# First attention of a four-stage block: the probabilities turned in 32x32 blocks on VectorE and exchanged through memory, with the order around the mixing changed

## Chip, cores and metric

One NeuronCore of one Trainium2 chip runs the whole program. The metric is the device time of one execution in microseconds (us), the median of three runs. TensorE has two clock levels, 1.2 and 2.4 GHz. A granted clock of 1.00 in the tables is the higher one.

## The reference

Sixteen tiles of 128 tokens with 512 features pass four residual stages, each behind a layer norm without gains. The change is in the first:

```
x = x + xattn(layernorm(x), ctx)           # 2048 tokens; this case
x = x + ffn(layernorm(x))                  # 512-1024-1024-512
x = x + xattn_rope(layernorm(x), ctx)
x = x + mlp_and_experts(layernorm(x))

def xattn(h, c):                           # H = 16 heads, D = 128; per batch row 128 queries, 128 keys
    q, k, v = h @ Wq, c @ Wk, c @ Wv       # 512x2048, 256x2048, 256x2048
    q, k = rmsnorm(q, gq), rmsnorm(k, gk)  # per head
    attn = softmax(q k^T / sqrt(D))
    return (attn @ v) @ Wo                 # 2048x512
```

All is float32. A large product is computed as three products of a rounded part (`_hi`) and a rest (`_lo`) of each operand.

## The kernel before

The first attention takes 32 steps, `s = 0..31`. The weights of 8 heads fit at a time, so steps 0 to 15 do the 16 tiles with heads 0 to 7, and steps 16 to 31 the same tiles with heads 8 to 15. In a step the 8 heads are two groups of `G = 4`, `g = 0, 1`. Each group fills one PSUM bank of 512 columns at each stage of the work. The second half of the weights comes in around steps 14 to 16: ScalarE writes the rounded part (`split_hi`), VectorE the rest (`split_lo`).

The order on each engine is written out by hand, one function `step(s)` for each, and semaphores join them (`at(name, s)` is the count that `name` has after step `s`). A step works on two tiles at once: scores, softmax, mixing and output for tile `s`, and keys, queries and values for tile `s + 1`. It also turns the normalised x of tile `s + 2`.

TensorE's order in a plain step is: `score(s,0)`, `output(s-1,1)`, `score(s,1)`, `keys(s+1,0)`, `turn_p(s,0)`, `keys(s+1,1)`, `mix(s,0)`, `queries(s+1,0)`, `turn_p(s,1)`, `queries(s+1,1)`, `mix(s,1)`, `output(s,0)`, `turn_x(s+2)`, `values(s+1,0)`, `values(s+1,1)`. A product of queries or an output is 12 matmuls of 128x512, one of keys or values is 6.

The path of one group through a step:
- `maxima` (VectorE) waits for `score` and gives the bias. `exps` (ScalarE) writes four heads of unscaled probabilities and their sums. `normalise` (VectorE) takes the reciprocal and multiplies.
- `turn_p` (TensorE) transposes the four 128x128 blocks into PSUM, `copy_pT` (VectorE) copies them to `pT_sb`, and `mix` multiplies with the values.
- `split_o` on ScalarE and then on VectorE makes `oT_hi` and `oT_lo` for `output`. The second group mixes into bank 1, in which the next `score(s+1,0)` writes, so that one waits for `oT_lo1`.

Queries and keys of tile `s + 1` are turned without TensorE: VectorE transposes 32x32 blocks (`turn_q`, `norm_and_turn_k`) into `blocks`, SyncE (SP) stores them to `turned` in HBM (`send`) and loads them back in another order (`bring`) as `qkT`. The norm of k needs its squares (`square` on ScalarE) and GpSimd's `mean`. `square` of q waits for `turn_q`, since both read the same bank.

SP issues its transfers in the order written, and a wait holds all that stand behind it.

Of the kernel before, what the change touches and what calls it, by code (L numbers as in the profile page):

```python
# [90 lines left out]
def l0_attention(place, sem, bank, ident, ident_in, x, ctxT, wq, wk, wv, wo, gq, gk, turned, x1):  # L91
# [14 lines left out]
    spots |= spots_of(200, "qkT1 4")  # L106
# [8 lines left out]
    def parts(name, shape):  # L115
# [21 lines left out]
    pT_sb = [sb(f"pT_sb{g}", [P, G * P], F32) for g in range(2)]  # L137
# [16 lines left out]
        s_turn y_begun y_ready y_added wq0_staged wv_staged wk_staged wq1_staged wo0_staged wo1_staged""".split()  # L154
    names += [f"{n}{g}" for g in range(2) for n in """q_made k_made v_made q_blocks k_blocks qk_stored qk_loaded v_copied q_squared
        k_squared q_rms k_rms scored bias_ready exped normed p_turned pT_copied mixed oT_hi oT_lo""".split()]
# [75 lines left out]
    def sync(sp, ahead):  # L232
# [33 lines left out]

        def step(s, second_half=True, storing=True):
# [111 lines left out]
    def tensor(pe, ahead):  # L379
# [63 lines left out]
        def step(s):  # L443
# [7 lines left out]
            if now == STEPS - 1:  # L451
                ahead["turn_x"](pe, 0, 3)
            if now == FIRST:
# [3 lines left out]
            if there(s):  # L457
                turn_p(s, 0)
            if there(s + 1):
                keys(s + 1, 1)  # L460
            if now == STEPS - 1:
                ahead["hidden1"](pe, 0, 0)
            if there(s):
                mix(s, 0)
            if there(s + 1):
# [3 lines left out]
            if there(s):  # L469
                turn_p(s, 1)  # L470
            if now == STEPS - 1:
                pe.wait_ge(*at("v_copied1", s))
                ahead["hidden1"](pe, 0, 1)
            if there(s + 1):
                queries(s + 1, 1)
            if there(s):
                mix(s, 1)
# [4 lines left out]
            if there(s):  # L482
                output(s, 0)
            if now == STEPS - 1:
                ahead["hidden1"](pe, 0, 2)
            if there(s + 2):
                turn_x(s + 2)
            if there(s + 1):
                values(s + 1, 0)
                values(s + 1, 1)  # L490
            if now == STEPS - 2:
# [7 lines left out]
    def scalar(act, ahead):  # L499
# [38 lines left out]
        def step(s):  # L538
# [20 lines left out]
            if now == FIRST:  # L559
                split_hi(act, "wq1", 0)  # L560
            if there(s):
# [4 lines left out]
            if now == NB - 1:  # L566
                split_hi(act, "wv0", 1)
                split_hi(act, "wv1", 1)
            if now in (0, NB):
                split_hi(act, "wo1", now // NB)  # L570
            if there(s + 1):
                square(s + 1, 0, "q")
            if now == NB - 2:
                split_hi(act, "wq0", 1)
            if now == FIRST:
                split_hi(act, "wv0", 0)
                split_hi(act, "wv1", 0)
            if now == STEPS - 2:
                ahead["split_x_hi"](act, 0, 0)
            if now == STEPS - 1:  # L580
                ahead["hidden_hi"](act, 0, 0, 0)
            if there(s + 1):
                square(s + 1, 1, "q")
# [4 lines left out]
            if now == STEPS - 2:  # L588
                ahead["split_x_hi"](act, 0, 1)
            if now == STEPS - 1:  # L590
                ahead["hidden_hi"](act, 0, 0, 1)
                ahead["split_hi"](act, 4)
            if there(s + 2):
                split_xT(s + 2)
# [14 lines left out]
    def vector(dve, ahead):  # L609
# [79 lines left out]
        def step(s, first_half=False):  # L689
# [8 lines left out]
            if there(s - 1):  # L698
                add_y(s - 1)
            if now == STEPS:  # L700
# [8 lines left out]
            if there(s):  # L709
                copy_pT(s, 0)  # L710
# [24 lines left out]
            if there(s):  # L735
                split_o(s, 0)
# [6 lines left out]
            if there(s):  # L743
                copy_pT(s, 1)
# [8 lines left out]
            if now == NB - 2:  # L753
# [1920 lines left out]
```

## Time and profile before

| | |
|---|---|
| median of 3 runs | 1987.45 us (1985.17 to 1993.48) |
| span of the profiled execution | 1985.1 us |
| TensorE matmul busy | 1935.9 us, 98% |
| VectorE busy | 1315.2 us, 66% |
| ScalarE busy | 742.2 us, 37% |
| GpSimd busy | 564.5 us, 28% |
| mean granted clock | 0.996 |
| first attention, first `score` to last `score` of group 0 | 30.77 to 724.93 us |

The span is the time from the first to the last instruction of one execution. An engine's share is a mean over four stages that differ, so it doesn't say what a change of one stage is worth. That has to be read in the steps of the stage. The 32 steps follow each other with the same pattern, so one step can be read for nearly all.

### The profile page before, as it was taken

What the parts mean: (1) busy time and instruction counts of PE and PEld (TensorE: products, weight loads), DVE (VectorE), ACT (ScalarE), POOL (GpSimd) and SP (SyncE); (2) the same over time, 40 slices, a digit from 0 to 9 for tenths busy, and PEclk for the clock granted to TensorE, in tenths of its full rate; (3) what the DMA queues carried; (4) which work ended last, traced back from release to release, by engine and by line L of the source; (5) the groups of instructions that cost most, each with busy time, mean ns of one, the idle gap of its engine ahead of it and who ended that gap; (6) DMA issues with size and microseconds to landing.
All of it is one profiled execution on the core that took longest, in us unless ns stands there. A gap on an engine that the chain in (4) does not pass through costs nothing. (4 is left out here: it accounts for less than half of the span.)

```text
span 1985.1 us, 35876 instructions
## 1 busy us (share of the span) xinstructions
PE 1935.9 (98%) x13552; PEld 1562.9 (79%) x13552; DVE 1315.2 (66%) x2493; ACT 742.2 (37%) x2275; POOL 564.5 (28%) x705
## 2 busy tenths in 40 slices
PE   6999999899999999999999899999999999999999
PEld 4888888778888878888888677777688888888887
DVE  6656655665555654343345599988868878888786
ACT  5555455654555543111122344444433222122211
POOL 3322222322223425310121343433310222322231
PEclk9999999999999999999999899999999999999999
DMA  6632333433444433020122100000112546555654
GB/s 233 221 103 90 99 114 108 165 112 117 137 148 143 144 107 128 27 80 32 32 69 93 63 28 18 21 23 19 54 54 70 191 154 210 192 192 167 201 163 160
DMA packets 126294, 222.39 MB, mean 112 GB/s; under 512 B 17392, under 2 KB 72688, under 8 KB 126192
## 3 DMA queue, kind: packets, MB, share of 16 engines
q1 hardware_dynamic: 102480, 134.01, 20.5%
q0 software_dynamic: 23712, 87.04, 13.2%
q8 instruction: 61, 1.00, 0.2%
q14 instruction: 41, 0.34, 0.1%
HBM read 170.16 MB, written 50.86 MB: 111 GB/s over the span
## 5 line engine op out<-in xcount | busy, mean ns | idle before, releaser
L2385 POOL DMA_INDIRECT m_ring<-in_table,m_row x128 | 127.3, 994 | 370.0 <-DVE l_x_all L2498 264.1
L48 PE MATMUL four_banks<-l_yT_hi,m_hi 128*128 128x512 f32 x512 | 199.4, 389 | 0.0
L48 PE MATMUL four_banks<-l_yT_lo,m_hi 128*128 128x512 f32 x512 | 199.2, 389 | 0.0
L1147 DVE TENSOR_SCALAR f_relu<-bank,f_b 128x512 f32<-128x512 f32 x64 | 48.0, 750 | 166.3 <-ACT f_h_hi L1090 166.3
L529 ACT ACTIVATE prob<-four_banks,mx,rms 128x128 f32<-128x128 f32 x256 | 114.0, 454 | 114.3 <-DVE mx L667 114.3
L328 POOL TENSOR_TENSOR rms<-ssq,constants 128x4 f32<-128x4 f32 x128 | 34.9, 273 | 391.9 <-ACT junk_k L518 237.9
L1090 ACT ACTIVATE f_h_hi<-bank,f_b 128x512 fp32r<-128x512 f32 x64 | 44.2, 690 | 255.6 <-PE bank L48 255.6
L331 POOL TENSOR_TENSOR rms<-rms,constants 128x4 f32<-128x4 f32 x128 | 130.1, 1016 | 10.0
L48 PEld LDWEIGHTS four_banks<-l_yT_hi,m_hi 128*128 128x128 f32 x512 | 96.1, 188 | 20.1 <-issue 0.2
L48 PEld LDWEIGHTS four_banks<-l_yT_lo,m_hi 128*128 128x128 f32 x512 | 96.1, 188 | 20.0
L2362 ACT ACTIVATE m_act_of<-m_dot,l_ln_y 128x2 f32<-128x2 f32 x64 | 19.0, 297 | 238.6 <-DVE m_junk L2488 238.6
L682 DVE TENSOR_TENSOR oT_lo<-four_banks,oT_hi 128x512 fp32r<-128x512 f32 x64 | 44.2, 691 | 95.5 <-ACT oT_hi L536 95.5
L48 PE MATMUL bank<-f_h_hi,f_w_hi 128*128 128x512 f32 x256 | 100.7, 394 | 1.0 <-DVE f_relu L1147 0.9
L48 PE MATMUL bank<-f_h_lo,f_w_hi 128*128 128x512 f32 x256 | 99.7, 389 | 0.0
L48 PE MATMUL bank<-m_hi,m_prod_hi 128*128 128x512 f32 x256 | 99.7, 389 | 0.0
L48 PE MATMUL bank<-f_h_hi,f_w_lo 128*128 128x512 f32 x256 | 99.7, 389 | 0.0
L2488 DVE SCALAR_TENSOR_TENSOR m_junk<-m_x_in,l_ln_y,m_ring 128x512 bf16<-128x512 f32 x128 | 92.0, 751 | 11.6 <-DMA m_ring<-in_table,m_row 10.5
L48 PE MATMUL four_banks<-l_yT_hi,m_gate 128*128 128x512 f32 x256 | 99.6, 389 | 0.0
L48 PE MATMUL bank<-m_hi,m_prod_lo 128*128 128x512 f32 x256 | 99.6, 389 | 0.0
L48 PE MATMUL four_banks<-l_yT_hi,m_up 128*128 128x512 f32 x256 | 99.6, 389 | 0.0
L48 PE MATMUL bank<-m_down,m_prod_hi 128*128 128x512 f32 x256 | 99.6, 389 | 0.0
L48 PE MATMUL four_banks<-wo_hi,oT_hi 128*128 128x512 f32 x240 | 99.4, 414 | 0.0
(316 smaller groups left out, 5410.2 us busy)
## 6 DMA issues: line engine op xcount, KB each, us to landing
turned<-blocks SPq DMA_DIRECT2D x64, 512.0 KB, 2.9
qkT<-turned SPq DMA_DIRECT2D x64, 512.0 KB, 4.3
f_stage<-in_w POOLq DMA_DIRECT2D x14, 512.0 KB, 4.6
f_x_in<-x SPq DMA_DIRECT2D x18, 256.0 KB, 3.5
ctx_in<-in_ctxT SPq DMA_DIRECT2D x32, 128.0 KB, 2.6
x_in<-in_x SPq DMA_DIRECT2D x16, 256.0 KB, 2.7
x<-xres SPq DMA_DIRECT2D x16, 256.0 KB, 2.1
x<-l_x_all SPq DMA_DIRECT2D x16, 256.0 KB
```

The costliest lines, as they stand in the source:

```text
L48: mm = pe.matmul(out, st, mv, start=first and n == 0, stop=last and n == len(terms) - 1)
L328: pool.tensor_tensor(rms[g][:, 1, own], ssq[g][:, 0 if of == "q" else 1, :], constants[:, 0, own], ALU.add).then_inc(S["eps_added"], 1)
L331: pool.tensor_tensor(rms[g][:, 0, own], rms[g][:, 1, own], constants[:, 1, own], ALU.pow).then_inc(S[f"{of}_rms{g}"], 1)
L529: a = act.activation(prob[g][:, j, :], bank[(1, 3)[g]][:, j * P:(j + 1) * P], ACT.Exp, bias=mx[g][:, 1, j:j + 1], scale=rms[g][:, 0, j:j + 1],
L682: dve.tensor_tensor(flat(oTp[g][1]), bank[(0, 1)[g]][:], flat(oTp[g][0]), ALU.subtract).then_inc(S[f"oT_lo{g}"], 1)
L1090: act.activation(out, bank[HB[m % 2]][:], ACT.Relu, bias=b12[:, layer, m:m + 1]).then_inc(S["h_hi"], 1)
L1147: dve.tensor_scalar(relu[m % 2][:], bank[HB[m % 2]][:], b12[:, layer, m:m + 1], 0.0, ALU.add, ALU.max).then_inc(S["relu_ready"], 1)
L2362: act.activation(act_of[:, t, k.start:k.stop], dot[:, t, k.start:k.stop], ACT.Silu, scale=ln[:, 2 * t + 1:2 * t + 2]).then_inc(S["silued"], 1)
L2385: pool.indirect_dma_start(ring[slot][:], None, table, bass.IndirectOffsetOnAxis(ap=row[:, tile_of(g), k:k + 1], axis=0)).then_inc(S[f"got{ ...
L2488: d = dve.scalar_tensor_tensor(junk[:, k % PER, :], x_in[t % 2][:], ln[:, 2 * t:2 * t + 1], ring[slot][:, 0:DM], ALU.subtract, ALU.mult, a ...
```

## The change

The probabilities are no longer turned by TensorE. ScalarE's `exps` writes the keys of a head in another order (key `4a + b` at place `32b + a`). VectorE's `normalise` then transposes 32x32 blocks into `dealt`. SP stores `dealt` to `shares` in HBM (`deal`) and loads it back in another order into `pT_sb` (`take`), which is laid out in four pieces of 32 queries. `turn_p` and `copy_pT` go.

The order changes with it. On TensorE the turn of the next x and `values(s+1,0)` stand ahead of `mix(s,0)`, `values(s+1,1)` between the mixings, and `output(s,0)` at the end. `output(s-1,1)` keeps its place. On ScalarE and VectorE both `split_o` come behind the work on tile `s + 1`, and so do some conversions of weights. `add_y` moves behind the second maxima. On SP, `deal` and `take` of each group stand ahead of `send` and `bring`.

```diff
@@ memory and names
+    spots |= spots_of(200, "qkT1 4 dealt 2")
-    pT_sb = [sb(f"pT_sb{g}", [P, G * P], F32) for g in range(2)]
+    dealt = sb("dealt", [P, 4, G, 32], F32)
+    pT_sb = [sb(f"pT_sb{g}", [P, 4, G, 32], F32) for g in range(2)]
+    shares = nc.dram_tensor("shares", (2, 4, P, P), F32).ap()
@@ SP
+        def deal(s, g):
+            sp.wait_ge(*at(f"p_blocks{g}", s))
+            sp.dma_start(shares[g].rearrange("p (j b) r -> (p j) (b r)", b=4), dealt[:].rearrange("p b h i -> p (b h i)")
+                         ).then_inc(S["p_stored"], 16)
+
+        def take(s, g):
+            sp.wait_ge(S["p_stored"], 16 * (2 * s + g + 1))
+            if there(s - 1):
+                sp.wait_ge(*at(f"mixed{g}", s - 1))
+            sp.dma_start(pT_sb[g][:].rearrange("k p h i -> k p (h i)"), shares[g].rearrange("p k r -> k p r")
+                         ).then_inc(S[f"p_loaded{g}"], 16)
...
                 load_ctx(s + 2)
+            if there(s):
+                deal(s, 0)
+                take(s, 0)
             if storing:
                 store(s - 1)
             if second_half and there(s + 3):
                 load_x(s + 3)
+            if there(s):
+                deal(s, 1)
+                take(s, 1)
@@ TensorE
         def queries(s, g):
...
+            elif there(s - 1):
+                pe.wait_ge(*at("exped1", s - 1))
         def values(s, g):
...
+            elif there(s - 1):
+                pe.wait_ge(*at("v_copied0", s - 1))
-        def turn_p(s, g):
-            pe.wait_ge(*at(f"normed{g}", s))
+        def mix(s, g):
+            pe.wait_ge(S[f"p_loaded{g}"], 16 * (s + 1))
+            pe.wait_ge(*at(f"v_copied{g}", s))
             if g == 0 and there(s - 1):
                 pe.wait_ge(*at("y_added", s - 1))
-            turn((0, 1)[g], flat(prob[g]), f"p_turned{g}")
-
-        def mix(s, g):
-            pe.wait_ge(*at(f"pT_copied{g}", s))
-            pe.wait_ge(*at(f"v_copied{g}", s))
             for j in range(G):
                 c = slice(j * P, (j + 1) * P)
-                mm = pe.matmul(bank[(0, 1)[g]][:, c], v_sb[g][:, c], pT_sb[g][:, c], start=True, stop=True)
+                out = bank[(0, 1)[g]][:, c].rearrange("d (p i) -> d p i", p=4)
+                mm = pe.matmul(out, v_sb[g][:, c], pT_sb[g][:, :, j, :], start=True, stop=True)
@@ ScalarE
             for j in range(G):
-                a = act.activation(prob[g][:, j, :], bank[(1, 3)[g]][:, j * P:(j + 1) * P], ACT.Exp,
+                scores = bank[(1, 3)[g]][:, j * P:(j + 1) * P].rearrange("q (a b) -> q a b", b=4)
+                a = act.activation(prob[g][:, j, :].rearrange("q (b a) -> q a b", b=4), scores, ACT.Exp,
@@ VectorE
-            dve.tensor_tensor(prob[g][:], prob[g][:], den[g][:, 1, :].unsqueeze(2).to_broadcast([P, G, P]),
-                              ALU.mult).then_inc(S[f"normed{g}"], 1)
-
-        def copy_pT(s, g):
-            dve.wait_ge(*at(f"p_turned{g}", s))
-            dve.tensor_copy(pT_sb[g][:], bank[(0, 1)[g]][:]).then_inc(S[f"pT_copied{g}"], 1)
+            then(dve.tensor_tensor(prob[g][:], prob[g][:], den[g][:, 1, :].unsqueeze(2).to_broadcast([P, G, P]), ALU.mult))
+            if g == 1 or there(s - 1):
+                dve.wait_ge(S["p_stored"], 16 * (2 * s + g))
+            dve.transpose(dealt[:], blocks_of(flat(prob[g]))).then_inc(S[f"p_blocks{g}"], 1)
```

The steps in the new order, each in a plain step and then in the odd ones (`now` is the step's number):

```
TensorE  score(s,0) output(s-1,1) score(s,1) keys(s+1,0) keys(s+1,1) queries(s+1,0) queries(s+1,1)
         turn_x(s+2) values(s+1,0) mix(s,0) values(s+1,1) mix(s,1) output(s,0)
ScalarE  exps(s,0) exps(s,1) square k0 k1 q0 q1 of s+1, split_xT(s+2) split_o(s,0) split_o(s,1)
         copy_v(s+1,0) copy_v(s+1,1) split_ctx(s+2)
         15: split_hi wv0, wv1 between the squares of q0 and q1
         14: split_hi wk0, wk1, wq0 between split_o(s,0) and split_o(s,1);  0 and 16: split_hi wo1 there
VectorE  maxima(s,0) normalise(s,0) maxima(s,1) add_y(s-1) layer_norm(s+2) normalise(s,1)
         norm_and_turn_k, turn_q of (s+1,0) and of (s+1,1), split_xT(s+2) split_o(s,0) statistics(s+3) split_o(s,1)
         15: split_lo wq1 and, 0 and 16: split_lo wo0, behind normalise(s,1), as before
         15: split_lo wv0 ahead of norm_and_turn_k(s+1,1);  14: split_lo wk0, wk1 behind split_o(s,0)
31       TensorE: the first two products of the next stage ahead of mix(s,0), the third between the mixings
```

## Rows read from the trace of the kernel before

**Rows 1.** Windows view of step 8: busy time of each engine, clock, DMA share.

```profile
187.94:210.00 22.06, 22.06 (x165) 17.95 (x164) 13.30 (x30) 11.18 (x54) 6.30 (x12) 1.00 0.31 100
```

**Rows 2.** Timeline of step 8, TensorE: start us, us, engine, line, tiles.

```profile
187.94 1.08 PE L420 MATMUL four_banks<-qkT 128*32 128x128 f32 x32
...
194.17 0.39 PE L48 MATMUL bank<-wk_hi,ctx_lo 128*128 128x512 f32 x1
194.40 0.60 PE L382 MATMUL four_banks<-ident,prob 128*128 128x128 f32 x4
...
195.07 0.40 PE L48 MATMUL bank<-wk_lo,ctx_hi 128*128 128x512 f32 x1
...
196.23 1.05 PE L434 MATMUL four_banks<-pT_sb,v_sb 128*128 128x128 f32 x8
...
210.00 1.08 PE L420 MATMUL four_banks<-qkT 128*32 128x128 f32 x32
```

**Rows 3.** Timeline of step 8, the other engines.

```profile
191.68 0.21 ACT L529 ACTIVATION_READ_ACCUMULATOR prob<-four_banks,mx,rms 128x1 f32 x1
...
193.55 0.69 DVE L664 TENSOR_REDUCE mx<-four_banks 128x4 f32<-128x512 f32 x1
...
194.47 0.46 ACT L529 ACTIVATE prob<-four_banks,mx,rms 128x128 f32<-128x128 f32 x1 [2.58 <-DVE mx L667]
...
196.23 0.28 ACT L518 ACTIVATE junk_k<-bank 128x128 bf16<-128x128 f32 x1
...
197.73 1.01 POOL L331 TENSOR_TENSOR rms<-rms,constants 128x4 f32<-128x4 f32 x1
...
199.53 1.12 DVE L657 SCALAR_TENSOR_TENSOR k_sb<-bank,rms,gains 128x128 f32<-128x128 f32 x4
...
204.27 0.67 DVE L650 STREAM_TRANSPOSE blocks<-four_banks 128x512 f32<-128x512 f32 x1
204.98 0.28 ACT L518 ACTIVATE junk_q<-four_banks 128x128 bf16<-128x128 f32 x1 [1.81 <-DVE blocks L650]
...
205.46 2.83 SPq L264 DMA_DIRECT2D qkT<-turned  x2
...
206.00 0.62 ACT L536 ACTIVATE oT_hi<-four_banks 128x512 fp32r<-128x512 f32 x1
...
206.65 0.69 DVE L682 TENSOR_TENSOR oT_lo<-four_banks,oT_hi 128x512 fp32r<-128x512 f32 x1 [1.70 <-ACT oT_hi L536]
```

**Rows 4.** Lines by form, and line 1901 with its shortest, median and longest ns.

```profile
L660 DVE STREAM_TRANSPOSE blocks<-k_sb 128x512 f32<-128x512 f32 x64 | 45.5, 711 | 2.2
L678 DVE COPY pT_sb<-four_banks 128x512 f32<-128x512 f32 x64 | 43.0, 673 | 22.3 <-PE four_banks L382 22.3
L2461 DVE TENSOR_TENSOR m_best<-m_best,m_total 128x32 f32<-128x32 f32 x4 | 0.8, 192 | 0.1
L1901 DVE TENSOR_SCALAR l_ang<-l_pos x4: 197/427/1276, 1040.4 to 1042.6; 128x32 f32<-128x32 f32 x4
```

**Rows 5.** DMA issues of the page: KB each, median us from issue to landing.

```profile
turned<-blocks SPq DMA_DIRECT2D x64, 512.0 KB, 2.9
qkT<-turned SPq DMA_DIRECT2D x64, 512.0 KB, 4.3
```

**Rows 6.** Timelines at steps 0, 1, 15, 16, and conversions by form.

```profile
30.77 1.08 PE L420 MATMUL four_banks<-qkT 128*32 128x128 f32 x32
...
55.58 1.08 PE L420 MATMUL four_banks<-qkT 128*32 128x128 f32 x32
...
365.01 1.08 PE L420 MATMUL four_banks<-qkT 128*32 128x128 f32 x32 [0.34 <-DMA qkT<-turned]
...
392.23 1.08 PE L420 MATMUL four_banks<-qkT 128*32 128x128 f32 x32 [2.87 <-DMA qkT<-turned]
...
L203 ACT ACTIVATE wv_hi<-stage 128x1024 fp32r<-128x1024 f32 x4 | 4.1, 1101 | 0.0
L207 DVE TENSOR_TENSOR wq_lo<-stage,wq_hi 128x2048 fp32r<-128x2048 f32 x3 | 6.9, 2287 | 1.6 <-ACT wq_hi L203 1.6
```

More of the change, by code:

```diff
@@ L88, in norm_statistics, with l0_attention @@
     then(rsqrt_steps(dve, then, ln[:, tiles, 1], ln_t[:, 0, tiles], ln_t[:, 1, tiles]))
-def l0_attention(place, sem, bank, ident, ident_in, x, ctxT, wq, wk, wv, wo, gq, gk, turned, x1):
+def l0_attention(place, sem, bank, ident, ident_in, x, ctxT, wq, wk, wv, wo, gq, gk, turned, shares, x1):
     H, D, HALF, G = 16, 128, 8, 4
@@ L153, in l0_attention @@
         g_loaded stats_ready ln_eps ln_ready xn_ready xT_turned xT_hi xT_lo ctx_hi ctx_split set stored eps_added
-        s_turn y_begun y_ready y_added wq0_staged wv_staged wk_staged wq1_staged wo0_staged wo1_staged""".split()
+        s_turn y_begun y_ready y_added p_stored wq0_staged wv_staged wk_staged wq1_staged wo0_staged wo1_staged""".split()
     names += [f"{n}{g}" for g in range(2) for n in """q_made k_made v_made q_blocks k_blocks qk_stored qk_loaded v_copied q_squared
-        k_squared q_rms k_rms scored bias_ready exped normed p_turned pT_copied mixed oT_hi oT_lo""".split()]
+        k_squared q_rms k_rms scored bias_ready exped p_blocks p_loaded mixed oT_hi oT_lo""".split()]
     PIECES = ("wq0", "wq1", "wk0", "wk1", "wv0", "wv1", "wo0", "wo1")
@@ L452, in step @@
                 ahead["turn_x"](pe, 0, 3)
+                ahead["hidden1"](pe, 0, 0)
+                pe.wait_ge(*at("v_copied1", s))
+                ahead["hidden1"](pe, 0, 1)
             if now == FIRST:
@@ L456, in step @@
                 keys(s + 1, 0)
-            if there(s):
-                turn_p(s, 0)
-            if there(s + 1):
                 keys(s + 1, 1)
[L461 to L465, printed above, removed]
                 queries(s + 1, 0)
@@ L468, in step @@
                 ahead["turn_x"](pe, 0, 0)
[L469 to L473, printed above, removed]
             if there(s + 1):
                 queries(s + 1, 1)
-            if there(s):
-                mix(s, 1)
             if now == STEPS - 2:
@@ L481, in step @@
                 ahead["turn_x"](pe, 0, 1)
[L482 to L485, printed above, removed]
             if there(s + 2):
@@ L489, in step @@
                 values(s + 1, 0)
+            if there(s):
+                mix(s, 0)
+            if there(s + 1):
                 values(s + 1, 1)
+            if now == STEPS - 1:
+                ahead["hidden1"](pe, 0, 2)
+            if there(s):
+                mix(s, 1)
+                output(s, 0)
             if now == STEPS - 2:
@@ L560, in step @@
                 split_hi(act, "wq1", 0)
+            if now == STEPS - 1:
+                ahead["hidden_hi"](act, 0, 0, 0)
+            if there(s + 1):
+                square(s + 1, 0, "q")
+            if now == NB - 1:
+                split_hi(act, "wv0", 1)
+                split_hi(act, "wv1", 1)
+            if now == FIRST:
+                split_hi(act, "wv0", 0)
+                split_hi(act, "wv1", 0)
+            if now == STEPS - 2:
+                ahead["split_x_hi"](act, 0, 0)
+            if there(s + 1):
+                square(s + 1, 1, "q")
+            if now == STEPS - 1:
+                ahead["hidden_hi"](act, 0, 0, 1)
+            if now == STEPS - 2:
+                ahead["split_x_hi"](act, 0, 1)
+            if there(s + 2):
+                split_xT(s + 2)
             if there(s):
@@ L565, in step @@
                 split_hi(act, "wk1", 1)
-            if now == NB - 1:
-                split_hi(act, "wv0", 1)
-                split_hi(act, "wv1", 1)
+                split_hi(act, "wq0", 1)
             if now in (0, NB):
                 split_hi(act, "wo1", now // NB)
[L571 to L583, printed above, removed]
             if now is not None and AHEAD_FROM < now <= AHEAD_FROM + 4:
@@ L697, in step @@
                 ahead["split_x_lo"](dve, 0, 2)
-            if there(s - 1):
+            if now == STEPS:
                 add_y(s - 1)
-            if now == STEPS:
                 ahead["hidden_lo"](dve, 0, 0, 2)
@@ L708, in step @@
                 ahead["split_x_lo"](dve, 0, 3)
-            if there(s):
-                copy_pT(s, 0)
+            if there(s - 1) and now != STEPS:
+                add_y(s - 1)
             if now == FIRST:
@@ L742, in step @@
                 split_lo(dve, "wq1", 0)
-            if there(s):
-                copy_pT(s, 1)
+            if now == NB - 1:
+                split_lo(dve, "wv0", 1)
             if there(s + 1):
@@ L765, in step @@
                 ahead["hidden_lo"](dve, 0, 0, 0)
-            if there(s):
-                split_o(s, 1)
+                ahead["hidden_lo"](dve, 0, 0, 1)
             if now == STEPS - 2:
@@ L773, in step @@
                 split_xT(s + 2)
+            if there(s):
+                split_o(s, 0)
+            if now == NB - 2:
+                split_lo(dve, "wk0", 1)
+                split_lo(dve, "wk1", 1)
+            if now in (0, NB):
+                split_lo(dve, "wo1", now // NB)
             if first_half:
                 statistics(s + 3)
+            if there(s):
+                split_o(s, 1)
             if now == NB - 2:
                 split_lo(dve, "wq0", 1)
-            if now == STEPS - 1:
-                ahead["hidden_lo"](dve, 0, 0, 1)
         all_steps(dve, step, first_half=True)
@@ L2578, in build @@
         done, programs0 = l0_attention(place, sem, bank, ident, a["ident"], a["x"], a["ctxT"], a["wq0"], a["wk0"], a["wv0"], a["wo0"],
-                                       a["gq"], a["gk"], turned, x1)
+                                       a["gq"], a["gk"], turned, shares, x1)
         over, ahead1, programs1 = l0_ffn(place, sem, bank, ident, done, x1, a["w1"], a["b1"], a["w2"], a["b2"], a["w3"], a["b3"], x2)
-        free = [s for n, s in done.items() if not n.rstrip("012345").endswith(("loaded", "staged", "stored"))]
+        free = [s for n, s in done.items() if not n.rstrip("012345").endswith(("loaded", "staged", "stored")) or n.startswith("p_")]
         over["semaphores"] = ranges_of([s.num for s in free])
```

14 lines of the change are left out of this document (removed).

## The prediction

> **What bounds the kernel now.** I read first the windows view of one plain step of the attention (step 8), to see which engine has no slack [rows 1]: TensorE is busy for the whole 22.06 us, VectorE for 13.30, ScalarE for 11.18, the DMA engines for 31%, at a granted clock of 1.00. Then TensorE's timeline of that step [rows 2]: it begins with a `score` at 187.94 and the next begins at 210.00; every later step up to the last has this 22.06, except those in which the second half of the weights is put in place. So in this stage only two things move the end: TensorE work taken out, and any wait put in. The weight loads and matmuls of a product follow each other every 0.23 us (194.17 to 194.40 is one such interval); a turn of four transposes at 194.40, with the next product's second matmul at 195.07, takes 0.67 less one interval of 0.23, that is 0.44 us. Last I read the timeline of the other engines in the same step [rows 3], because the new order only pays if they deliver as early as TensorE then asks. Below, t is the time after the step's first `score` (187.94).
>
> **What leaves TensorE.** Two `turn_p` a step: 2 x 0.44 = 0.88 us. What TensorE alone would then need is 22.06 - 0.88 = 21.18 us. The mixing reads its moving operand in four pieces of 32 columns; `score` already reads `qkT` in that form, and I price this at nothing. The products that are moved keep their cost.
>
> **What VectorE gets.** Two copies of 0.67 go, two 32x32-block transposes of 0.71 come [rows 4], so its sum stays. Only their places matter. The first transpose takes the time that `add_y` had in front of the second maxima: exps 0 end at t = 3.95 (191.68 + 0.21), reciprocal, product and transpose bring VectorE to about t = 5.6, and `maxima(s,1)` began at t = 5.61 before. So exps 1 still begin at t = 6.53, the squares of k at 8.29, and GpSimd's power for k ends at 10.80 [rows 3].
>
> **The chain that then decides.** `norm_and_turn_k(s+1,0)` began at t = 11.59, directly behind other VectorE work (its row shows no idle time). The first split of o leaves that place, so it can begin when GpSimd is done, at 10.85. From there to the second `turn_q` were 4.74 us (199.53 to 204.27), 0.6 of them `copy_pT`, which goes: 4.14. The second q blocks begin at 14.99 and are ready at 15.70 (before: 17.04, the start of ScalarE's squares at 204.98). ScalarE's queue is now squares of q 1, split of xT, split of o 0. The squares occupy 1.02 us (204.98 to 206.00), so xT begins at 16.72. Two 512-element activations of 0.62 in a row I space at 0.5, since the end of one overlaps the next: o 0 begins at 17.22 and is out at 17.87. VectorE subtracts xT meanwhile and then o 0 in 0.69: `oT_lo0` is there at about 18.65, and `output(s,0)` begins at 18.7. TensorE would be ready for it at 21.18 - 12 x 0.23 - 0.09 = 18.33. It waits 0.4 us. The new period is 18.7 + 2.76 + 0.09 = 21.55 us, a gain of **0.5 us a step** instead of 0.88. The second half of o follows in time: mixing 1 ends at about 18.5, and its low part is out near 20.2, before the next `score` at 21.55.
>
> **The exchange through memory.** The block transpose of g = 1 ends at t = 10.1. The store is 256 KB, half of `turned`; the issues of SP land after 2.9 us for the 512 KB store and 4.3 for the 512 KB load back [rows 5]. I take 2.4 + 3.6, with the full 2.9 + 4.3 as the upper bound and nothing as the lower: the probabilities land at 16.2, at most 17.4, and mixing 1 is due at 17.4 (its matmuls of 1.05 end at 18.5, row 196.23). For g = 0 the blocks are ready at 5.7, landed at 12 to 13, due at 15.2. Hidden, without a margin at the upper bound. On SP, `take(s,1)` holds the queue until about 12.6 + 0.5. Behind it stands `send(s+1,0)`, whose blocks are ready at 13.4, so it loses nothing. The second `send` and the first `bring` go out at 15.8 and 16.3 instead of 17.1 and 17.5 (205.46), and q and k land near 20.6, before the `score` at 21.55. The time that SP waits for each store delays `store` and `load_x` only, which nobody waits for closely.
>
> **The other new waits.** The second transpose waits until the first store has read `dealt`: landed at t = 8.1, asked for at 9.4. `queries(s+1,1)` waits for exps 1, done at 8.4, asked for at about 10.6. `values(s+1,0)` waits for a copy of the step before. None costs anything; the first would hold VectorE, and all of the k and q work behind it, from a store of 3.7 us on.
>
> **The exps.** They now write with a step of 32 elements (128 bytes). No ScalarE row shows such a write. Lower bound: nothing. Upper bound: the elements take twice their time. A square of 128 elements takes 0.28 and an activation of 512 takes 0.62 [rows 3], so 128 elements are (0.62 - 0.28)/3 = 0.11 us, on top of 0.46. Eight exps stand in the chain (four in front of `maxima(s,1)`, four behind), so that bound adds 0.88 us to the period. The nearest row is on VectorE: line 1901 writes 32 elements with a step of 16 bytes in 197 ns at its shortest, and a 32-element operation with contiguous output takes 192 [rows 4]. Doubled it would be 33 ns more, and it is 5. I take nothing.
>
> The Trainium skill (SBUF — State Buffer, "Door 1: The DMA port swizzle") says that SBUF works in lines of 16 bytes, and that each access which crosses to a new line pays. Every element of the new write does that. By it the sum would be the upper bound instead of nothing, and the change would lose; the VectorE row speaks against it for writes, and no row here tests ScalarE.
>
> **Steps that are not plain.** In three steps around the half the weights are replaced, and the change moves these conversions too. Before, the step from 365.01 to 392.23 took 27.22, 5.2 too much, for a late `qkT` [rows 6]; its three neighbours lost 1.5 together (periods of 22.25, 22.46 and 22.98) and step 0 2.75 (its first `score` at 30.77, the next at 55.58): 9.5 in all. In the new order I estimate:
> - step 14: three conversions (1.1 us for each half of `wk` as for `wv` [rows 6], about 1.9 for `wq` with twice the elements) stand ahead of the second split of o, which the next `score` needs. It comes at about 22.9, 1.3 late.
> - step 15: `wv` is converted behind the squares of q 0, which wait for q blocks that come at 15.5, behind `wq1_lo` (2.29 us, VectorE). `values` wants it at 13.9 and gets it at 17.7. `wv0_lo` stands ahead of the second k, the second q blocks come at 21.3, output 0 at 24.3: 5.5 lost. The late `qkT` is hidden behind that.
> - step 16: `wo0_lo` (of the same size) ahead of k: 2.5. Step 0 alike, 4.
>
> Together 13.3 against 9.5: 4 lost. In the first steps weights and exchange share the DMA engines, 2 us. In the last step the mixings wait for their transfers with little in front of them, 1 us.
>
> **Sum.** 28 plain steps x 0.5 = -14; +4, +2, +1: **-7 us**. The profiled execution spans 1985.1 us, the median of the runs is 1987.45 (2.3 around the span and within the spread of 8 us), so **1980 us**, within 0.5% (10 us, about what a measurement of this kernel can tell from no change). Its own range: 1973 to 1988.
>
> **Rivals.**
> 1. *Slower: the scattered write of the exps.* Place: the eight exps ahead of the squares of k. Each 0.01 us of an exp costs 0.08 a step. From 0.46 to 0.52 the plain step is back at 22.06, and with the 7 us of the odd steps the kernel is slower than before from about 0.03 us per exp. At the upper bound the period is 22.43: 28 x 0.37 = +10, +7: 2005 us. For it: every exp is ahead of everything. Against: the VectorE row.
> 2. *TensorE stays the bound.* If GpSimd or the two ScalarE instructions behind the last squares come 0.4 us earlier than I put them, the whole 0.88 counts: 28 x 0.88 = 25, less 7: 1969 us. Against it: each link is a row of this step.
> 3. *The probabilities come late.* It decides where store and load of g = 1 need over 7.3 us from the transpose. 1 us later than that puts output 0 at 19.2, the period at 22.1, and only the odd steps count: 1995 us. For it: the loads in steps with weight traffic. Against: the DMA engines are busy for 31% in a plain step.
>
> **Chances.** Forecast 0.50, rival 1 0.27 (spread over 1990 to 2006), rival 2 0.13, rival 3 0.10. Faster than 1977.5: rival 2 and a quarter of the forecast, 0.26. Slower than 1997.4: two thirds of rival 1 and a fifth of rival 3, 0.20. Between: 0.54. The range 1966 to 2005 takes in all bounds but the ends of the tails.
>
> **What the new profile should show.** A plain step of 21.5 to 21.6 us between first `score`s. No row of `turn_p`. TensorE idle 0.3 to 0.5 us once a step, ahead of `output(s,0)`, released by VectorE's `oT_lo`. ScalarE's exps at 0.46 us (rival 1: 0.5 or more). No idle time ahead of the mixings with a DMA as releaser (rival 3). Steps 14 to 16 as 23, 27 and 24 us. I am wrong if the exps are longer, if the mixings wait for the transfer, or if the wait ahead of `output(s,0)` is absent.

## The result, and the profile after

| | before | after |
|---|---|---|
| median of 8 runs each | 1989.44 us (1985.17 to 1993.48) | 1999.02 us (1995.17 to 2001.48) |
| span of the profiled execution | 1985.1 us | 1999.7 us |

The ratio of after to before is 1.0039, 95% interval 1.0028 to 1.005: slower by some 8 us, where 0.4% faster was forecast. The profiled execution took 2001.48 us, at the upper end of its runs, so its 14.6 us of longer span overstate the loss, but they show where it lies.

From the page after: the exps of part 5 (busy us, mean ns of one, idle before), then the issues of part 6 (KB each, median us to landing).

```profile
L542 ACT ACTIVATE prob<-four_banks,mx,rms 128x128 f32<-128x128 f32 x256 | 121.7, 582 | 184.1 <-DVE mx L680 184.1
...
turned<-blocks SPq DMA_DIRECT2D x64, 512.0 KB, 3.2
qkT<-turned SPq DMA_DIRECT2D x64, 512.0 KB, 4.1
shares<-dealt SPq DMA_DIRECT2D x64, 256.0 KB, 2.0
pT_sb<-shares SPq DMA_DIRECT2D x64, 256.0 KB, 2.8
```

The windows view after, columns as in [rows 1]: a plain step of the first half (8), one of the second half (18), and step 30, the last before the last.

```profile
212.69:234.37 21.68, 21.37 (x158) 17.25 (x157) 13.35 (x30) 10.96 (x54) 6.28 (x11) 1.00 0.46 149
441.83:464.03 22.20, 21.47 (x157) 17.25 (x157) 12.79 (x28) 10.96 (x54) 5.52 (x9) 1.00 0.50 162
...
704.67:737.17 32.50, 24.80 (x165) 19.77 (x165) 14.69 (x32) 11.27 (x54) 6.45 (x12) 0.89 0.37 126
```

In step 8 TensorE is busy for 0.7 us less than in [rows 1], and idle for 0.3 us. Step 30 has almost 8 us without TensorE, and a lower mean clock. (Counted from the first `score` at 30.77, the plain step of [rows 1 to 3] is step 7; plain steps are alike, and here is step 8.)

With the starts of the first `score` of each step in TensorE's timelines, the 14.6 us fall apart like this. "Start to `score(0,0)`" is the time from the span's start, the last line that from `score(31,0)` to the span's end.

| stretch | before | after | difference |
|---|---|---|---|
| start to `score(0,0)` | 30.77 | 31.83 | +1.1 |
| steps 0 and 1 | 46.87 | 51.17 | +4.3 |
| steps 2 to 12 | 242.85 | 238.06 | -4.8 |
| steps 13 to 17 | 116.78 | 120.77 | +4.0 |
| steps 18 to 29 | 264.73 | 262.84 | -1.9 |
| step 30 | 22.93 | 32.50 | +9.6 |
| `score(31,0)` to the end | 1260.17 | 1262.53 | +2.4 |

So the change pays in the plain steps, 0.44 us a step in the first half and 0.16 in the second, and one step costs more than all of them give. The table holds one execution of each kernel. Its rows of steps 0 and 1 and of 13 to 17 differ by up to 3 us among the kernels of the experiments, even where their order in these steps is the same; step 30 takes 31.5 to 33.0 us in all of them that leave its order as it is.

**Step 8.** The timeline of step 8 after (start us, us, engine, line, tiles): exps, the k norm, the second q blocks, and then the first split of o. I take t from 212.69 here.

```profile
214.77 0.58 ACT L542 ACTIVATE prob<-four_banks,mx,rms 128x128 f32<-128x128 f32 x1 [3.40 <-DVE mx L680]
215.22 0.57 ACT L542 ACTIVATE prob<-four_banks,mx,rms 128x128 f32<-128x128 f32 x1
...
216.44 0.22 ACT L542 ACTIVATION_READ_ACCUMULATOR prob<-four_banks,mx,rms 128x1 f32 x1
...
223.56 1.12 DVE L670 SCALAR_TENSOR_TENSOR k_sb<-bank,rms,gains 128x128 f32<-128x128 f32 x4 [0.60 <-POOL rms L350]
...
227.71 0.68 DVE L663 STREAM_TRANSPOSE blocks<-four_banks 128x512 f32<-128x512 f32 x1
228.42 0.28 ACT L530 ACTIVATE junk_q<-four_banks 128x128 bf16<-128x128 f32 x1 [1.21 <-DVE blocks L663]
...
229.43 0.61 ACT L516 ACTIVATE xT_hi<-four_banks 128x512 fp32r<-128x512 f32 x1
229.91 0.62 ACT L549 ACTIVATE oT_hi<-four_banks 128x512 fp32r<-128x512 f32 x1
...
230.69 0.68 DVE L693 TENSOR_TENSOR oT_lo<-four_banks,oT_hi 128x512 fp32r<-128x512 f32 x1
...
231.42 0.50 PE L48 MATMUL four_banks<-wo_hi,oT_hi 128*128 128x512 f32 x1 [0.31 <-DVE oT_lo L693]
```

Each link of the forecast chain is here: the k norm at t = 10.87 (forecast 10.85), the second q blocks at 15.02 (14.99), the squares at 15.73 (15.70), xT at 16.74 (16.72), o 0 at 17.22 (17.2), `oT_lo0` out at 18.68 (18.65), and TensorE idle for 0.31 us in front of `output(8,0)`, released by it.

**Step 30.** The timeline after, of the load, of VectorE and of TensorE in step 30.

```profile
725.76 0.50 SPq L895 DMA_DIRECT2D f_x_in<-x  x1
...
729.92 0.69 DVE L1135 BATCH_NORM_STATS2 f_bn<-f_x_in 128x6 f32<-128x512 f32 x1 [6.78 <-DMA f_x_in<-x]
...
730.75 1.25 DVE L693 TENSOR_TENSOR oT_lo<-four_banks,oT_hi 128x512 fp32r<-128x512 f32 x2
...
731.46 0.79 PE L48 MATMUL four_banks<-wo_hi,oT_hi 128*128 128x512 f32 x1 [7.10 <-DVE oT_lo L693]
...
732.05 0.63 PE L48 MATMUL four_banks<-wo_lo,oT_hi 128*128 128x512 f32 x1
...
732.48 0.63 PE L48 MATMUL four_banks<-wo_hi,oT_lo 128*128 128x512 f32 x1
```

VectorE takes the statistics of tile 3 for the stage that follows (`ahead["statistics"](dve, 0, 3)`). In the changed order this call stands ahead of both `split_o`. Its load is issued at 725.76, behind the last `bring`, and VectorE waits 6.78 us for it; both low parts of o stand behind, and TensorE waits 7.10 us for them. In the kernel before, the same wait begins in step 30 too, but there the call stood behind both splits, and no TensorE work of that step waited for it (in step 31 TensorE waits 1.0 us for probabilities):

```profile
726.91 0.69 DVE L1127 BATCH_NORM_STATS2 f_bn<-f_x_in 128x6 f32<-128x512 f32 x1 [4.59 <-DMA f_x_in<-x]
```

When TensorE starts again, its matmuls follow each other every 0.43 us (732.05 to 732.48) and not every 0.23: the lower of its two clock levels. The windows view of this stretch, in which the granted clock is 0.56:

```profile
731.46:737.17 5.71, 5.71 (x16) 4.38 (x17) 0.54 (x1) 0.00 (x0) 0.27 (x1) 0.56 0.00 0
```

From the start of this output to the next `score` are 5.71 us, and 2.95 in step 8 (231.42 to 234.37). So the wait costs 7.1 us and the slower matmuls some 2.8; experiment 1, which has neither, takes 9.7 us less for this step.

TensorE's waits from the start to 780 us, after (us in total, times, longest).

```profile
PE four_banks L48 <- DVE oT_lo L693: 14.5, 26, 7.1
...
PE four_banks L443 <- DMA qkT<-turned: 9.4, 8, 4.6
...
PE four_banks L454 <- DMA pT_sb<-shares: 0.2, 1, 0.2
```

The mixings (L454) wait for the exchanged probabilities once, for 0.2 us.

### The profile page after: what moved, and what is told of

Its sections match the earlier page's. It is cut to its first block and busy times, and to the rows that moved or that the text cites. A ratio compares the mean times of both kernels' runs of the same rounds, so it can differ in the third digit from the quotient of the medians.

```text
span 1999.7 us, 35630 instructions
## 1 busy us (share of the span) xinstructions
PE 1921.9 (96%) x13296; PEld 1544.7 (77%) x13296; DVE 1321.3 (66%) x2493; ACT 735.0 (37%) x2275; POOL 559.4 (28%) x705
## 5 line engine op out<-in xcount | busy, mean ns | idle before, releaser
L542 ACT ACTIVATE prob<-four_banks,mx,rms 128x128 f32<-128x128 f32 x256 | 121.7, 582 | 184.1 <-DVE mx L680 184.1
L347 POOL TENSOR_TENSOR rms<-ssq,constants 128x4 f32<-128x4 f32 x128 | 28.0, 219 | 419.6 <-ACT junk_k L530 298.5
L677 DVE TENSOR_REDUCE mx<-four_banks 128x4 f32<-128x512 f32 x64 | 43.0, 672 | 94.2 <-PE four_banks L443 94.2
```

The source lines that it names most:

```text
L347: pool.tensor_tensor(rms[g][:, 1, own], ssq[g][:, 0 if of == "q" else 1, :], constants[:, 0, own], ALU.add).then_inc(S["eps_added"], 1)
L542: a = act.activation(prob[g][:, j, :].rearrange("q (b a) -> q a b", b=4), scores, ACT.Exp, bias=mx[g][:, 1, j:j + 1], scale=rms[g][:, 0, j ...
L677: then(dve.tensor_reduce(mx[g][:, 0, :], bank[(1, 3)[g]][:].rearrange("p (h k) -> p h k", h=G), AX.X, ALU.max))
```

## The experiments

All nine kernels start from the changed one. Ratios are to the kernel before, run on the same chip, with a 95% interval. Periods are from first `score` to first `score`.

**1. The statistics of step 30 behind the second split of o.**

```diff
@@ VectorE
-            if now == STEPS - 2:
-                ahead["statistics"](dve, 0, 3)
             if there(s + 2):
                 split_xT(s + 2)
...
             if there(s):
                 split_o(s, 1)
+            if now == STEPS - 2:
+                ahead["statistics"](dve, 0, 3)
```

> The changed kernel with one move: in step 30 VectorE takes the statistics of the next stage's fourth x tile behind the second split of o instead of ahead of the first. Theory (a wait at the seam makes the slowdown): in the changed kernel VectorE sits 6.78 us in front of that instruction until its load lands, and output(30,0) on TensorE waits 7.1 us for it. Without that the interval between the first scores of steps 30 and 31 falls from 32.5 us to 22.5 to 24, and the time by 7 to 10 us, to a ratio of 0.999 to 1.001 against before. Rival (the load stays the bound, since the layer norm and the turn of that tile at the start of step 31 wait for it too): the wait moves to the turn ahead of keys or to the first products of step 31, and less than 3 us are gained.

Measured: 1991.72 us (1988.8 to 1996.32), ratio 1.0016 [1.0002, 1.0031], above the 0.999 to 1.001 that was expected, whose upper end lies in the interval; the profiled span is 1987.0. Step 30 goes from 32.50 to 22.82 us. In VectorE's timeline of this kernel neither low part of o waits for a load any more.

```profile
718.97 0.69 DVE L693 TENSOR_TENSOR oT_lo<-four_banks,oT_hi 128x512 fp32r<-128x512 f32 x1
...
720.96 0.69 DVE L693 TENSOR_TENSOR oT_lo<-four_banks,oT_hi 128x512 fp32r<-128x512 f32 x1 [1.30 <-ACT oT_hi L549]
```

The cause of step 30 is shown: one call in a queue. The plain steps stay at 21.68. The ratio moves by less than 9.7 us would (0.0023, or 4.6 us, from two intervals that leave room for 0 to 9.6). A small part of the wait moves, as the rival had it: the first product of the next stage waits 3.1 us for its turned x, 1.5 after.

**2. The store and load of x behind the exchange.** In the second half SP also issues `store(s-1)` and `load_x(s+3)`, in the change between the first `take` and the second `deal`.

```diff
@@ SP
+            if there(s):
+                deal(s, 1)
+                take(s, 1)
             if storing:
                 store(s - 1)
             if second_half and there(s + 3):
                 load_x(s + 3)
-            if there(s):
-                deal(s, 1)
-                take(s, 1)
```

> The changed kernel with one move on SyncE: the store of x and the load of the next x stand behind the exchange of group 1 instead of ahead of it. Theory (in steps 16 to 31 the two transfers in front lengthen the store of the probabilities, SyncE comes later to the first send of q and k, and the score waits for qkT): the mean period of steps 18 to 30 falls from 21.90 us to that of the first half, 21.67, the time by 2 to 4 us. Rival (the DMA engines are simply busier in the second half, or SyncE has one issue more): the period stays within 0.1 us.

Measured: 2008.78 us (2007.97 to 2009.38), ratio 1.0086 [1.0059, 1.0113]. The forecast was wrong: steps 18 to 29 take 22.68 us on average where after has 21.90, the first half stays at 21.73. From the DMA view of 440 to 700 us of this kernel (issues, KB each, median us to landing):

```profile
turned<-blocks SPq DMA_DIRECT2D x22, 512.0 KB, 4.5
qkT<-turned SPq DMA_DIRECT2D x22, 512.0 KB, 4.3
shares<-dealt SPq DMA_DIRECT2D x23, 256.0 KB, 2.0
```

The store of the probabilities is quick again (2.0 us; the median in this stretch after is 2.5, over stores with and without the transfers of x in front). But now the two transfers of x go out just ahead of the `send`s, which take 4.5 us at the median (3.7 after), and `bring`, on which the next `score` waits, goes out later (in step 18 at t = 19.0, and 18.4 after). TensorE's waits from 440 to 700 us, first after, then in this kernel (us in total, times, longest):

```profile
PE four_banks L443 <- DMA qkT<-turned: 3.9, 6, 1.7
...
PE four_banks L443 <- DMA qkT<-turned: 11.0, 11, 1.2
```

The same line has 7.5 us in 10 times in experiment 4, and in experiment 5 there is none. So the place of these two transfers matters by some 0.8 us a step. That named the third place to try, experiment 5.

**3. The exps in natural order.** This kernel leaves out the permutation of the keys: exps write contiguous elements. The rest is unchanged.

```diff
@@ ScalarE, exps
-                scores = bank[(1, 3)[g]][:, j * P:(j + 1) * P].rearrange("q (a b) -> q a b", b=4)
-                a = act.activation(prob[g][:, j, :].rearrange("q (b a) -> q a b", b=4), scores, ACT.Exp,
+                a = act.activation(prob[g][:, j, :], bank[(1, 3)[g]][:, j * P:(j + 1) * P], ACT.Exp,
...
```

> The changed kernel with the exps writing each head in natural order, without the step of 32 elements. The permutation of the keys is left out with it, so the mixing pairs probabilities and values wrongly; every other instruction is the same. Theory (the scattered write lengthens an exp, 0.58 us against 0.46, but the next exp still starts 0.44 us later, so only the last of each four is late): exps at 0.46 us, the plain period of 21.67 us shorter by at most 0.1, the time by 0 to 3 us. Rival (each exp costs its 0.12 us in the chain): the period falls by up to 8 x 0.12 = 1.0 us, bounded by TensorE's own 21.2, that is by 0.4 to 0.5, and the time by 10 us or more.

Measured: 1996.44 us (1993.54 to 2000.26), ratio 1.0028 [1.0015, 1.0042], which overlaps that of the changed kernel. The exps on its page:

```profile
L541 ACT ACTIVATE prob<-four_banks,mx,rms 128x128 f32<-128x128 f32 x256 | 113.8, 454 | 180.7 <-DVE mx L679 180.7
```

and in ScalarE's timeline the exps of group 1 of the same step:

```profile
215.12 0.46 ACT L541 ACTIVATE prob<-four_banks,mx,rms 128x128 f32<-128x128 f32 x1 [2.60 <-DVE mx L679]
...
215.57 0.45 ACT L541 ACTIVATE prob<-four_banks,mx,rms 128x128 f32<-128x128 f32 x1
...
216.78 0.21 ACT L541 ACTIVATION_READ_ACCUMULATOR prob<-four_banks,mx,rms 128x1 f32 x1
```

A single exp is 0.13 us shorter, near the upper bound of rival 1 (0.11), but the four of group 1 take 1.87 us here (215.12 to 216.99) and 1.91 with the step of 32 elements (219.27 to 221.18 after), those of group 0 take 1.86 and 1.89: the exps start every 0.44 us in both. The period stays at 21.66. Rival 1 is out.

**4. The first split of o ahead of the split of x.**

```diff
@@ ScalarE, and the same on VectorE
-            if there(s + 2):
-                split_xT(s + 2)
             if there(s):
                 split_o(s, 0)
+            if there(s + 2):
+                split_xT(s + 2)
```

> The changed kernel with the first split of o ahead of the split of the next xT, on ScalarE and on VectorE. Theory (the chain q blocks 1, squares of q 1, split of xT, split of o 0 makes TensorE wait 0.3 us ahead of output(s,0)): that wait vanishes in plain steps of the first half, their period falls from 21.67 to 21.2 to 21.3 us, the time by 6 to 11 us. In the second half qkT becomes the later one and the gain is smaller there. Rival (something else is as late, for instance the second split of o or qkT for the next score): the wait moves to the score, and the period falls by less than 0.1 us.

Measured: 1990.41 us (1985.65 to 1995.24), ratio 0.9993 [0.9977, 1.0008]. In the first half the plain step is 21.12 us, the wait in front of `output(s,0)` is gone. TensorE alone is the bound, and the two turns are worth 22.06 - 21.12 = 0.94 us. In step 8 `output(s,0)` begins at t = 18.18, and at 18.73 after: the wait costs 0.55 us, though its row after shows 0.31. That row counts TensorE as busy for all 1.05 us of the mixing in front, while here the output begins 0.81 us after the mixing does (225.93 to 226.74). In the second half the step is 21.9 on average: there `score`s wait for `qkT`, ten times from 440 to 700 us.

**5. The store and load of x at the end of SP's step.**

```diff
@@ SP
-            if storing:
-                store(s - 1)
-            if second_half and there(s + 3):
-                load_x(s + 3)
...
                 bring(s + 1, 1)
+            if storing:
+                store(s - 1)
+            if second_half and there(s + 3):
+                load_x(s + 3)
```

> The changed kernel with one move on SyncE, the other way round than in e2_sp: the store of x and the load of the next x stand behind the last bring of the step, so no transfer of x is ahead of the exchange or of the sends. Theory (in the second half the two transfers lengthen the store of the probabilities that SyncE then waits for, and every send and bring behind it is late by as much): the mean period of steps 18 to 30 falls from 21.90 us to 21.65 to 21.75, no score waits for qkT in most of these steps, and the time falls by 2 to 3 us. Rival (the amount of traffic counts, not its place): the loads of q and k, which now run beside the transfers of x, take longer, and the period stays at 21.9 or rises.

Measured: 1996.58 us (1994.9 to 1997.81), ratio 1.0037 [1.0022, 1.0052]. Steps 18 to 29 take 21.68 us on average, plain steps of the first half 21.73: the difference between the halves is gone, as expected, and no `score` of these steps waits for `qkT`. SP's timeline of step 18 after:

```profile
450.82 0.39 SPq L255 DMA_DIRECT2D x<-xres  x1
451.47 0.37 SPq L244 DMA_DIRECT2D x_in<-in_x  x1
452.12 0.33 SPq L270 DMA_DIRECT2D shares<-dealt  x1
455.81 0.37 SPq L277 DMA_DIRECT2D pT_sb<-shares  x1
456.29 1.63 SPq L260 DMA_DIRECT2D turned<-blocks  x2
460.20 1.76 SPq L265 DMA_DIRECT2D qkT<-turned  x2
```

and the same stretch of step 18 in experiment 5:

```profile
449.27 0.33 SPq L270 DMA_DIRECT2D shares<-dealt  x1
451.29 0.37 SPq L277 DMA_DIRECT2D pT_sb<-shares  x1
452.40 2.67 SPq L260 DMA_DIRECT2D turned<-blocks  x2
455.45 2.59 SPq L265 DMA_DIRECT2D qkT<-turned  x2
458.42 0.39 SPq L255 DMA_DIRECT2D x<-xres  x1
459.43 0.37 SPq L244 DMA_DIRECT2D x_in<-in_x  x1
```

From the second store of the probabilities to its load are 3.69 us after (452.12 to 455.81) and 2.02 here, since two transfers of 256 KB were given out just ahead of it; SP waits for the store, and both `send`s stand behind. The 12 x 0.22 = 2.6 us that these steps give back in the profile are 0.0013 of the time, less than the half width of the interval, and step 15 took 0.96 us more in this profile (29.07 against 28.11): the periods show this effect, the ratio can't.

**6. The conversions of weights at other places.** On ScalarE `wk`, `wv` and `wo1` go ahead of the squares of q 0, and `wq0` behind the second split of o. On VectorE `wk` and `wo0` go behind the second q blocks, and `wo1` behind the second split of o. The core of it:

```diff
@@ ScalarE
-            if there(s + 1):
-                square(s + 1, 0, "q")
+            if now == NB - 2:
+                split_hi(act, "wk0", 1)
+                split_hi(act, "wk1", 1)
             if now == NB - 1:
                 split_hi(act, "wv0", 1)
                 split_hi(act, "wv1", 1)
+            if now in (0, NB):
+                split_hi(act, "wo1", now // NB)
+            if there(s + 1):
+                square(s + 1, 0, "q")
...
@@ VectorE
-            if now in (0, NB):
-                split_lo(dve, "wo0", now // NB)
...
+            if now == NB - 2:
+                split_lo(dve, "wk0", 1)
+                split_lo(dve, "wk1", 1)
+            if now in (0, NB):
+                split_lo(dve, "wo0", now // NB)
...
             if there(s):
                 split_o(s, 1)
+            if now in (0, NB):
+                split_lo(dve, "wo1", now // NB)
```

> The changed kernel with the conversions of weights of steps 0, 14, 15 and 16 in other places. ScalarE: wk, wv and wo1 ahead of the squares of q 0, wq0 behind the second split of o. VectorE: wk and wo0 behind the second turn of q, wo1 behind the second split of o. Theory (the conversions stand in the chain to the splits of o): steps 14, 15 and 16, 22.78, 28.11 and 23.98 us, become about 22.0, 26 and 22.5, step 0 loses 1 to 2 us less, and the time falls by 4 to 7 us. Rival (the late qkT, from traffic of the weight loads, bounds these steps as it did before the change): step 15 stays over 27 us and less than 2 us are gained in all.

Measured: 1989.36 us (1985.9 to 1992.39), ratio 1.0004 [0.9993, 1.0016]. Step 0 takes 22.00 us (27.00 after), steps 14 to 16 take 22.04, 26.39 and 21.95 (22.78, 28.11, 23.98). Step 0 differs from run to run with the same order of these calls (24.71 in experiment 3, 26.85 in experiment 1), so its gain isn't sized by one profile. Nor is that of step 15, which took 27.19 to 29.07 us in experiments 1 to 5; but 26.39 lies below them all, and so do 25.68 and 25.91 in experiments 7 and 9. Steps 14 and 16 were 22.75 to 22.80 and 23.92 to 24.00 in each of experiments 1 to 5. In this kernel the `score` of step 16 waits 2.25 us for a late `qkT`.

**7. Experiments 1, 4, 5 and 6 together.**

> The moves of e1_stat, e4_o_first, e5_sp_end and e6_conv together. Theory (each wait is a matter of order, and TensorE alone needs 21.18 us a step against 22.06 before): plain steps at 21.1 to 21.2 us in both halves, the seam at 22.8, and a time of 1964 to 1973 us, a ratio of 0.987 to 0.992. Rival (qkT is the next bound, 0.4 us behind, as in the second half of e4_o_first): periods of 21.5 to 21.9 in the second half and a ratio of 0.993 or more.

Measured: 1967.58 us (1966.86 to 1967.83), ratio 0.9891 [0.9871, 0.9911]: faster than both kernels. The windows view of its step 8 and of its step 19:

```profile
206.69:227.81 21.12, 21.12 (x158) 17.16 (x157) 13.35 (x30) 10.98 (x54) 6.30 (x12) 1.00 0.46 154
444.16:465.28 21.12, 21.12 (x157) 17.16 (x156) 12.80 (x28) 10.98 (x54) 5.55 (x10) 1.00 0.54 180
```

TensorE is busy for the whole step in both halves. Steps 14 to 16 take 21.44, 25.68 and 21.39 us, step 30 takes 22.84. The single ratios below 1.0039 add up to 0.0106 (0.0023, 0.0046, 0.0002 and 0.0035), together they give 0.0148. The intervals of all these ratios are too wide to tell the two apart; the periods show it. In steps 18 to 29 experiment 4 alone leaves 21.9 us on average and 5 alone 21.7, all together 21.2 (21.12 in nine of the twelve): behind either wait stands the other.

**8 and 9. A second buffer for `dealt`.** In step 1 after, VectorE's second transpose waits for the first store, as these rows of the timeline show.

```profile
64.51 0.34 SPq L270 DMA_DIRECT2D shares<-dealt  x1
...
71.44 0.36 SPq L277 DMA_DIRECT2D pT_sb<-shares  x1
71.52 0.71 DVE L689 STREAM_TRANSPOSE dealt<-prob 128x512 f32<-128x512 f32 x1 [3.38 <-DMA shares<-dealt]
```

```diff
-    dealt = sb("dealt", [P, 4, G, 32], F32)
+    dealt = [sb(f"dealt{g}", [P, 4, G, 32], F32) for g in range(2)]
@@ VectorE, normalise
-            if g == 1 or there(s - 1):
-                dve.wait_ge(S["p_stored"], 16 * (2 * s + g))
+            if there(s - 1):
+                dve.wait_ge(S["p_stored"], 16 * (2 * s + g - 1))
...
```

> The changed kernel with a buffer dealt for each group (that of group 0 lies in the place of oT0_hi, which is unused then), so that the second block transpose does not wait for the first store to have read its source. Theory (in step 1 the weight loads slow the first store, the transpose stands 3.4 us behind it, and all k and q work of VectorE with it): the 3.38 us of idle time go, step 1 falls from 24.17 us to 21.6 to 22.5, the time by 1.5 to 2.5 us; no change in plain steps. Rival (SyncE has the same wait in take of group 0, ahead of deal 1, take 1 and the sends): the mixing of group 1 or the next score is late instead, and step 1 keeps more than 23 us.

> The moves of e7_all with the two buffers of e8_two. Theory: step 1 falls from 24.27 us to 21.2 to 22, the rest is as in e7_all, 1965 to 1967 us. Rival (SyncE's wait takes its place): as e7_all, 1967 to 1968 us.

Measured: experiment 8 (this alone) 1994.71 us (1990.49 to 1997.46), ratio 1.0024 [1.0011, 1.0037]; experiment 9 (with all of experiment 7) 1969.99 us (1966.31 to 1971.6), ratio 0.9897 [0.9877, 0.9917], no better than experiment 7. With the buffer alone the transpose doesn't wait, but step 1 stays at 24.34 us (24.17 after), because SP's queue waits for the same store. SP's waits from 50 to 85 us in experiment 8:

```profile
SPq L278 <- DMA shares<-dealt: 8.9, 2, 6.3
```

SP waits up to 6.3 us for a store of 256 KB in `take`, and everything of SP stands behind. As the rival had it, the mixing of group 1 then waits 1.16 us for its probabilities in step 1, and the next `score` 1.42 us for `qkT`. In experiment 9 step 1 takes 23.38 us and step 2 21.58, against 24.27 and 21.14 in experiment 7.

## Why the prediction was wrong

**What leaves TensorE; the chain that then decides: right.** Forecast 21.18 us for TensorE alone and 21.55 with the wait; measured 21.12 (experiment 4) and 21.56 to 21.68 in steps 2 to 12, with every link up to `oT_lo0` within 0.03 us. Only the end was off: TensorE could begin the output at t = 18.18 and not at 18.33, so the wait costs 0.55 us where the forecast has 0.37. Rival 2 (the whole gain at once) did not come, but one exchange of two calls makes it.

**The failed step: "In the last step the mixings wait for their transfers with little in front of them, 1 us".** It cost 9.6 us, for another reason. The diff moved the statistics of the next stage, with their wait for a load, ahead of both splits of o in step 30. The prediction costed this move nowhere: the list of steps that are not plain has the conversions alone, and "every later step up to the last has this 22.06" passes over step 30 with its 22.93. The rows of that step held the warning, VectorE's wait of 4.59 us for this load. Experiment 1 shows it: with the call moved back, step 30 takes 22.82 us. The mixings of step 30 wait for no transfer. Put into the sum, 9.6 in place of 1 makes -7 into +2; the next two points are most of the rest.

**"The time that SP waits for each store delays `store` and `load_x` only, which nobody waits for closely": wrong in the reverse direction.** It asked who waits for these two and not what they do to their neighbours. In steps 18 to 29 the gain is 0.16 us instead of 0.5. Experiments 2 and 5 show that their place alone makes the period 22.68, 21.90 or 21.68, through the wait of `score` for `qkT`.

**The steps around the half and the first two: right in kind, too small in this profile.** Steps 14, 15 and 16 were forecast as 23, 27 and 24 us and are 22.78, 28.11 and 23.98. One row of TensorE's waits from 366 to 395 us bears the forecast for step 15 out: `values` waits for the converted `wv`, forecast 3.8.

```profile
PE bank L58 <- ACT wv_hi L204: 3.0, 1, 3.0
```

Ahead of it the queries wait 1.5 us for `wq_lo`, which the forecast had at nothing, so `values` begins at t = 18.6 and not at 17.7, and output 0 at 25.2 and not at 24.3. Steps 13 and 17, taken as plain, are 22.54 and 23.36. By the forecast periods steps 13 to 17 were to take 117.05 us (22.85 + 27.05 + 24.05 + 2 x 21.55) against 116.78; they take 120.77. Steps 0 and 1 were to take 49.1 (21.55 + 4, 21.55, and 2 for the shared DMA engines) against 46.87; they take 51.17. Part of both misses belongs to this one execution: with the same order of the conversions (experiments 1 to 5 and 8) steps 13 to 17 take 117.95 to 120.54 us, with 13 at 21.57 to 22.73 and 17 at 21.60 to 22.71, and steps 0 and 1 take 48.45 to 51.15. The prediction also counts step 12 with its 22.25 as a neighbour of step 15, which changes nothing. Experiment 6 gives back 0.0035 of the time by moving the same calls once more.

**The exchange through memory: right, and cheaper.** Store 2.0 and load 2.8 us at the median, taken as 2.4 and 3.6. Rival 3 is out: 0.2 us of waiting in 780. The exception is step 1, where the wait that was priced at nothing "from a store of 3.7 us on" came (3.38 us); experiments 8 and 9 show that without it SP's own wait sets the step.

**The exps: nothing was the right value, for a wrong reason.** The row of VectorE that decided it was no guide: on ScalarE the scattered write makes an exp 582 ns long instead of 454. But the next exp starts 0.44 us after the one before in both orders, so the chain pays 0.03 to 0.04 us for a group of four. By the Trainium skill (SBUF — State Buffer, "Door 1: The DMA port swizzle") each access that crosses to a new line of 16 bytes pays; the trace agrees in the duration of one exp and not in the chain, and no run shows that the lines are the reason. "From about 0.03 us per exp" on the kernel was to lose; that took duration for cost.

**What stays open.** The 2.4 us behind the first `score` of step 31 (in experiment 7 even more: the first product of the next stage waits 3.8 us for its turned x, 1.5 after) were not tested. The 1.1 us ahead of the first `score` can't be told from no change: this stretch takes 29.46 to 31.84 us in the profiles of the experiments. Of steps 0 and 1 the waits are seen, their shares are not separated: step 0 alone runs between 24.7 and 27.0 us with its conversions in the same order (experiments 1 to 5 and 8). Nor is it known how steps 0, 1 and 13 to 17 of the kernel before differ from one execution to the next, since only one was profiled.

## What to carry to other kernels

When an order written by hand is changed, list every call that changed places in every step, those for the next stage and those under a condition too, and ask of each what it waits for and who stands behind it; one such call cost more than 23 plain steps gained. Ask of a transfer not only who waits for it, but also which transfer it shares the DMA engines with. A longer instruction costs a chain only what its successor starts later.

## What the runs showed that was not expected

- From a 256 KB store of `dealt` to the load that waits for it are 2.0 us, 3.3 at the median with two 256 KB transfers issued just ahead (group 1 in steps 18 to 29 after, 3.69 in step 18) and 6.9 in step 1 (64.51 to 71.44), where loads of weights run too. From 440 to 700 us a 512 KB store of `blocks` lands after 2.9 us at the median in experiment 7, and after 4.5 in experiment 2, where the same two go out just ahead of the stores.
- An activation of 128x128 that writes with a step of 128 bytes takes 582 ns against 454, and starts as often: the extra time lies where the next one overlaps.
- After 7.10 us of idle time TensorE came back at the lower clock level, at a granted clock of 0.56, and the output and the rest up to the next `score` took 2.8 us longer. After the 0.3 us waits of the plain steps the granted clock is 1.00.
